# Two routed layers take their last rows in the order of arrival, and VectorE rotates the first two groups of a second attention

## What is computed

```
x += 0.5 * routed(LN(x))      # "routed0"
x += attn0(LN(x))             # low rank: state and action of 32, one head, causal
x += 0.5 * routed(LN(x))      # "routed1", the same weights
x += 0.5 * gated(LN(x))       # ternary weights with scales, 704 inner columns
x += attn1(LN(x))             # 16 heads of 128, rope, causal
x += 0.5 * gated(LN(x))
```

```
def routed(x):                # 16 experts, the best 4 of each token, at most 128 tokens per expert
    scores = softmax(x @ gate_w.T)
    topk_w, topk_i = top_k(scores, 4);  topk_w /= topk_w.sum(-1)
    ...                       # buf: for each expert the numbers of its tokens, wbuf: their weights
    xg   = xpad[buf]
    mid  = silu(xg @ w_gate) * (xg @ w_up)
    eout = (mid @ w_down) * wbuf[..., None]
    y    = zeros.at[buf].add(eout)
    shared = (silu(x @ sw_gate) * (x @ sw_up)) @ sw_down
    return y + shared

def rope(x):                  # on q and k of attn1
    x1, x2 = split(x, 2)
    return concat([x1 * c + x2 * s, -x1 * s + x2 * c])
```

## Time and profile before

| | us |
|---|---|
| median of three runs | 2019.42 |
| lowest and highest | 2014.98, 2020.13 |
| the profiled execution | 2020.47 |
| its span in the trace | 2018.7 |
| mean granted clock of TensorE in it | 0.992 |
| TensorE busy | 1938.0 (96%) |
| VectorE busy | 1435.0 (71%) |
| ScalarE busy | 1316.5 (65%) |
| GpSimd busy | 936.9 (46%) |

### The profile page before, as it was taken

The page is one execution under the profiler, slowest core; times in us unless marked ns, Lnnn a source line. Parts: engine busy times, 40 slices in busy tenths (PEclk is TensorE's granted clock), DMA queues, the critical chain, the costliest instruction groups (busy, mean ns, idle before and its releaser), DMA issues.

```text
span 2018.7 us, 40238 instructions
## 1 busy us (share of the span) xinstructions
PE 1938.0 (96%) x13726; PEld 1763.0 (87%) x13726; DVE 1435.0 (71%) x3587; ACT 1316.5 (65%) x3367; POOL 936.9 (46%) x961
## 2 busy tenths in 40 slices
PE   7988989898999999999999999999999999999999
PEld 5768867787899999999999999999999999998888
DVE  8368763755878777787877778787777878777753
ACT  4336633444778777777877777787777778776752
POOL 2641126444454536555453645545364554536242
PEclk9999989999999999999999999999999999999999
DMA  7750068500000000000000000000000000000000
GB/s 267 219 100 1 33 195 209 144 1 9 9 9 6 10 6 4 7 9 9 6 9 7 4 7 9 9 7 9 7 4 7 9 9 7 9 6 1 22 27 32
DMA packets 58600, 73.44 MB, mean 36 GB/s; under 512 B 9760, under 2 KB 45216, under 8 KB 58272
## 3 DMA queue, kind: packets, MB, share of 16 engines
q1 hardware_dynamic: 48032, 58.03, 8.9%
q0 software_dynamic: 10368, 12.85, 3.8%
HBM read 51.06 MB, written 19.80 MB: 35 GB/s over the span
## 4 chain that ended last, share of the span: by engine, by line
PE 61%; DVE 12%; ACT 9%; issue 7%; POOL 7%; DMA 4%; SPq 0%; ACTq 0%; POOLq 0%; DVEq 0%
PE phase_scores L1242 16%; PE phase_ring L1300 9%; PE phase_y L167 5%; PE phase_y L166 5%; PE phase_y L165 5%; PE phase_ring L165 4%; PE phase_ring L167 4%; PE phase_ring L166 4%; ACT phase_p L1274 3%; DMA y_rows<-phase_out,phase_rows 3%; DVE phase_scores L1253 2%; POOL phase_rot L2474 1%; POOL phase_straight L2472 1%; PE phase_up_ps L165 1%; PE phase_up_ps L167 1%
## 5 line engine op out<-in xcount | busy, mean ns | idle before, releaser
L1274 ACT ACTIVATE phase_p<-phase_scores,phase_bias 128x512 f32<-128x512 f32 (+3 forms) x680 | 417.5, 628 | 117.3 <-DVE phase_bias L1262 116.7
L1320 DVE TENSOR_TENSOR phase_pt_lo<-phase_ring,phase_pt_hi 128x512 fp32r<-128x512 f32 (+3 forms) x680 | 390.7, 604 | 90.1 <-ACT phase_pt_hi L1315 86.2
L1315 ACT ACTIVATE phase_pt_hi<-phase_ring 128x512 fp32r<-128x512 f32 (+3 forms) x680 | 343.1, 536 | 105.1 <-PE phase_ring L1300 100.8
L1300 PE MATMUL phase_ring<-sb_ident,phase_p 128*128 128x128 f32 x2312 | 340.7, 274 | 12.1 <-ACT phase_p L1274 6.7
L165 PE MATMUL phase_y<-phase_pt_hi,phase_v_hi 128*128 128x256 f32 (+1 forms) x1152 | 341.3, 296 | 6.5 <-DVE phase_y_lo L2448 6.3
L167 PE MATMUL phase_y<-phase_pt_hi,phase_v_lo 128*128 128x256 f32 (+1 forms) x1152 | 321.3, 279 | 0.0
L166 PE MATMUL phase_y<-phase_pt_lo,phase_v_hi 128*128 128x256 f32 (+1 forms) x1152 | 321.2, 279 | 0.0
L1300 PEld LDWEIGHTS phase_ring<-sb_ident,phase_p 128*128 128x128 f32 x2312 | 271.8, 140 | 53.3 <-ACT phase_p L1274 16.9
L1255 DVE TENSOR_REDUCE phase_peaks<-phase_scores 128x1 f32<-128x512 f32 (+1 forms) x408 | 265.8, 666 | 45.8 <-PE phase_scores L1242 43.5
L2472 POOL TENSOR_TENSOR phase_straight<-phase_rot,late_rope 64x512 f32<-64x512 f32 x128 | 163.7, 1279 | 275.5 <-ACT phase_rot L2341 275.4
L2489 POOL TENSOR_TENSOR sb_x<-sb_x,phase_part 128x512 f32<-128x512 f32 x128 | 164.8, 1288 | 253.4 <-ACT phase_part L2376 247.0
(11 more groups left out here) (282 smaller groups left out, 4848.8 us busy)
## 6 DMA issues: line engine op xcount, KB each, us to landing
phase_e_up<-expert_up SPq DMA_DIRECT2D x32, 352.0 KB, 4.7
phase_e_dn<-expert_down SPq DMA_DIRECT2D x32, 256.0 KB, 5.0
y_rows<-phase_zero SPq DMA_DIRECT2D x16, 512.0 KB, 7.8
xn_rows<-phase_ln_xn SPq DMA_DIRECT2D x8, 512.0 KB, 2.9
sb_x<-y_rows POOLq DMA_DIRECT2D x8, 512.0 KB, 6.6
late_raw_qk<-qk SPq DMA_DIRECT2D x16, 256.0 KB, 2.7
sb_x<-x SPq DMA_DIRECT2D x4, 512.0 KB, 5.6
phase_e_up<-y_rows SPq DMA_DIRECT2D x4, 512.0 KB, 4.5
```

Of the source, the lines that this page charges most:

```text
L1274: act.activation(self.p[:, at:at + width], self.scores[:, at:at + width], ACT.Exp, bias=self.bias[:, t % 2:t % 2 + 1], accum_out=self.sums ...
L1300: done = pe.transpose(bank[:, j * P:(j + 1) * P], self.p[:, (4 * place + j) * P:(4 * place + j + 1) * P], self.core.ident[:])
L1315: act.activation(hi, value, ACT.Copy).then_inc(*self.t_hi.one)
L1320: dve.tensor_tensor(lo, value, as_f32(hi), ALU.subtract).then_inc(*self.t_lo.one)
```

## The change

Five things change in the stages around the routed layers and in the opening of the second attention.

1. `AMONG, BEHIND` go from 6, 12 to 4, 14: two steps of the shared expert move from among the experts to behind them. The results get six rooms instead of four, so the weighing of n waits for scatter n-6. The two new rooms lie in memory that held `raw_dn` (first stage) or is new (second).
2. The tail is put in the order of arrival: SyncE fetches chunk 0 from both arrays, then chunk 1; `grow` follows that order, and the second array of chunk 1 is added after the sums of chunk 3 have begun. The norm of chunk 0 stays in the tail; of chunk 1 only the measuring does. Scaling and transposing chunk 1 become the follower's work: in Attention0 before its second projection, in Gated among its first pieces (`GROWN_NORM`), whose norms of chunks 2 and 3 come a few pieces later.
3. GpSimd in Attention0 and in the first Gated waits for the rows of chunk 1 before it issues any of the adding DMAs.
4. At the start of routed1 TensorE does piece `up` 0 right after `gate` 0 and `gate` 1 before the last logits are turned back; ScalarE does the rows of chunk 3 before the copies of logits. `rank` stands behind `gate` 2 there, before it stood in front.
5. In the second attention VectorE does the rotation (`rotate`) and the low parts (`part_qk`) for head 0, groups 0 and 1 (`OPENING`); the other 126 groups stay with GpSimd.

The core of the diff:

```diff
-    AMONG, BEHIND = 6, 12
+    AMONG, BEHIND = 4, 14
...
+        more_out = self.raw_dn[:, 0:2, :] if start else sb("out_more", [P, 2, H])[:]
+        self.out_rooms = [self.out[:, n, :] for n in range(4)] + [more_out[:, n, :] for n in range(2)]
...
-        among = {("sums", 1, 1): [("ahead", 0)], ("round", last - 3): [("ahead", 1), ("ahead", 2)], ("up", last - 2): [("ahead", 3), ("grow", 0, 0)],
-                 ("round", last - 2): [("grow", 1, 0)], ("up", last - 1): [("grow", 0, 1), ("measure", 0)], ("up", last): [("grow", 1, 1)],
-                 ("round", last): [("scale", 0)], ("sums", NCH - 2, 1): [("measure", 1), ("flip", 0, 0), ("flip", 0, 1)],
-                 ("sums", NCH - 1, 0): [("scale", 1)], ("sums", NCH - 1, 1): [("flip", 1, 0), ("flip", 1, 1)]}
+        among = {("up", last - 3): [("ahead", 0)], ("sums", 1, 1): [("ahead", 1)], ("round", last - 3): [("ahead", 2)], ("up", last - 2): [("ahead", 3)],
+                 ("round", last - 2): [("grow", 0, 0)], ("up", last - 1): [("grow", 0, 1), ("measure", 0)], ("round", last): [("grow", 1, 0), ("scale", 0)],
+                 ("sums", NCH - 2, 1): [("flip", 0, 0), ("flip", 0, 1)], ("sums", NCH - 1, 0): [("grow", 1, 1)], ("sums", NCH - 1, 1): [("measure", 1)]}
...
-        for b in range(2):
+        for c, b in ((0, 0), (0, 1), (1, 0), (1, 1)):
             sp.wait_ge(*self.placed[b][tag, NE - 2 + b])
-            for c in range(2):
-                rows = core.y_rows[b][c * CH:(c + 1) * CH, :]
-                sp.dma_start(self.y_rooms[c][b], rows.rearrange("(t p) h -> p t h", p=P)).then_inc(*self.y_fetched[c][b].one)
...
         if not self.start:
             self.pe_gate(pe, 0)
+            self.pe_multiplier(pe, 0)
...
         self.pe_logits(pe, 3)
+        if not self.start:
+            pe.wait_ge(*self.logits_out[tag, 2])
+            self.pe_gate(pe, 1)
         self.pe_logits_back(pe, (2, 3))
...
             elif what == "flip":
-                pe.wait_ge(*self.acted[tag, NCH * ISM - 1])
-                self.first.pe_flip(pe, *key, self.first_banks[key[0]][key[1]])
+                self.first.pe_flip(pe, *key, self.first_banks[key[1]])
...
-                if n >= 4:
-                    dve.wait_ge(*self.placed[n % 2][tag, n - 4])
+                if n >= 6:
+                    dve.wait_ge(*self.placed[n % 2][tag, n - 6])
...
     def pool(self, pool):
+        pool.wait_ge(*self.first.normed_v[self.tag, 1])
         for step in self.order:
...
+            pool.wait_ge(*self.first.normed_v[tag, 1])
             self.prior.pool_grow(pool, 0)
             self.prior.pool_grow(pool, 1)
...
-            order += [("rows", nc)] * (nc > 1) + [("bias", nc)]
+            order += [("rows", nc), ("bias", nc)]
...
-    GROWN_NORM = {(1, 0): [("scale", 0, 2)], (1, 1): [("turn", 0, 2)], (1, 3): [("scale", 0, 3)], (1, 4): [("turn", 0, 3)]}
-    GROWN_LATE = {(0, 4): [("measure", 0, 2), ("invert", 0, 2)], (1, 0): [("measure", 0, 3), ("invert", 0, 3)]}
+    GROWN_NORM = {(0, 1): [("scale", 2, 1)], (0, 2): [("turn", 2, 1)], (1, 2): [("scale", 0, 2)], (1, 3): [("turn", 0, 2)],
+                  (1, 4): [("scale", 0, 3)], (1, 5): [("turn", 0, 3)]}
+    GROWN_LATE = {(1, 0): [("measure", 0, 2), ("invert", 0, 2)], (1, 1): [("measure", 0, 3), ("invert", 0, 3)]}
...
+    OPENING = ((0, 0), (0, 1))
...
+                if key in self.OPENING:
+                    dve.wait_ge(*self.crossing[key])
+                    self.rotate(dve, key)
+            elif what == "finish" and key in self.OPENING:
+                self.part_qk(dve, key)
...
+    def rotate(self, engine, key):
+
+        wide = self.wide(slice(0, 64), key[1])
+        engine.wait_ge(*self.rotated[key])
+        engine.tensor_tensor(self.straight[:], self.rot[0:64], wide, ALU.mult).then_inc(*self.straightened.one)
+        engine.wait_ge(*self.straightened[key])
+        engine.tensor_tensor(self.rot[0:64], self.straight[:], self.crossed[:], ALU.add).then_inc(*self.turned_by_rope.one)
```

81 lines of the change are left out of this document (44 added, 37 removed).

## The result

| | us |
|---|---|
| before, median of five runs | 2018.71 |
| after, median of five runs (2026.58 to 2031.58) | 2029.88 |
| ratio, with its 95% interval | 1.006 (1.0047 to 1.0072) |
| the profiled execution after, its span | 2030.73, 2028.9 |

The forecast was 2017.3 with a range of 2008 to 2025. It missed by 12.6 us, to the slow side.

A forecast was written before the change was run, and what follows sets the result against it. TensorE, busy 96% of the span, was taken as the bound. Terms 0.3 + 3.6 - 0.7 - 1.1 = 2.1 us won, off the 2019.42 median, gave 2017.3, range 2008 to 2025.

The forecast's parts named there:

- first tail and Attention0: First routed tail through Attention0's opening: 3.6 us won less a 3.3 stall, net +0.3, bounds -5.8 and +3.6.
- opening of routed1: Start of the second routed stage: 3.1 us from TensorE's gaps and 0.5 from the clock, +3.6 won.
- second tail and gated stage: Second routed tail and gated stage: 3.9 us ahead from upstream, only 3.2 left later, so -0.7; bounds -6.8 and +2.2.
- rotation: Second attention's opening: first score some 1.8 us earlier, but VectorE's later statistics delay the softmax; -1.1, bounds -2.5 and +1.8.
- What bounds the kernel now: Whole kernel: TensorE is busy 96%; the change touches only stretches holding some 27 us of idle or low-clock time.
- Chunk 1 leaves the tail: First tail and Attention0: first projection about 6.0 us earlier; with 1.0 more, less 2.7 and 0.7, 3.6 won.
- GpSimd's new wait takes most of this back: Attention0: late additions of y make VectorE stand 3.3 us before the statistics of chunk 2.
- Rooms at nothing, two pieces at 1.0: First routed tail: six rooms win 0; two pieces behind the experts cut the gap before piece 11 to 2.7, winning 1.0.
- The bound of 5.1: Second routed stage's opening: upper bound of the gain in us, if the whole low-clock stretch goes.
- C: Rival: late additions of y land slowly, 12.7 us each, each stage 6.1 longer, 2029.5; decides from about 7.7; chance 0.15.

The follow-up runs named there:

- e13: e12 with the rows of chunk 1 scaled ahead of both values products in Attention0; 2012.98 us, 0.9979 to before.
- e14: e13 with the transposes of chunk 1 also ahead of the second values product in Attention0; 2011.34 us, 0.9969 to before.
- e8: The changed kernel with GpSimd's wait undone in Attention0 only, kept in the first gated stage; 2029.31 us, 1.0047 to before.
- e1: The changed kernel with GpSimd's waits for the rows of chunk 1 undone in Attention0 and the first gated stage; 2024.16 us, 1.0040 to before.
- e5: e1 with the rows of y fetched and added in the old order; 2024.05 us, 1.0032 to before.
- e9: e5 with chunk 1 scaled and turned in routed1's own tail and the gated stage's tables as before; 2018.77 us, 0.9998 to before.
- e7: The kernel before with the new opening of routed1 and six rooms for results; 2015.42 us, 0.9989 to before.
- e6: The kernel before with AMONG, BEHIND set to 4, 14 alone; 2016.56 us, 0.9994 to before.
- e2: The changed kernel with scaling and turning of chunk 1 back in the tails, and GpSimd's wait gone; 2031.45 us, 1.0072 to before.
- e12: e9 with the rotation of the first groups back on GpSimd; 2015.57 us, 0.9993 to before.
- e10: The kernel before with the new opening of routed1 and AMONG, BEHIND at 4, 14; 2015.63 us, 0.9989 to before.
- e3: The kernel before with the opening of routed1 alone, including the moved rank and gate 2; 2014.94 us, 0.9990 to before.

## Why the prediction was wrong, point by point

In the terms of the sum, after against before by the two traces: first tail and Attention0 +0.3 forecast and -4.7 measured, opening of routed1 +3.6 and +3.9, second tail and gated stage -0.7 and -7.5, rotation -1.1 and -1.5. The first and the third term are the miss.

- **"What bounds the kernel now" held.** Outside the six stretches little moved: the first fetch of routed0 came 0.8 later, and from the first turned chunk of Attention1 to the end it took 1513.1 before and 1513.4 after.
- **"Chunk 1 leaves the tail": this step failed, in the sentence "VectorE paces the opening of the attention, so of 6.0 + 1.0 I take off 2.7 and 0.7 for shifted waits".** It charged the norm of chunk 1 in the follower as VectorE's own time, and dropped the 1.94 of transposes that it had named. In the trace VectorE's time is 2.6, as I had it, but the stretch grew by 8.1, since rows, transposes, high and low parts and projection follow one another from VectorE and ScalarE to TensorE and back, each waited for the last, and the clock fell. e13 and e14 show that it was largely the place: the same work in another place costs less by 2.6 and 4.2 (medians). The gain in front is less certain: the first projection (139.40 before) came 2.2 earlier in the trace of after, 4.2 in e8 and 5.1 in e1, which have the same tail, and 5.8 in e5 with the old order of rows, where I had 6.0. The wait before chunk 0's transposes doesn't explain the 2.2: it is 2.57 there and 5.14 and 4.49 in e8 and e1. What does is open.
- **"Second tail and gated stage", -0.7: failed by 7.** This is the largest error. I took the same moves for the same small price and followed the queues only to the piece at 397.02, where I found the whole 3.2 ahead. Measured are +1.0 in front and -8.5 in the stage: 0.6 to 3.0 of it is GpSimd's wait (after and e8 against e1 and e5), the rest chunk 1's norm among the pieces together with the later norms of chunks 2 and 3 (e5 against e9, 8.7).
- **"GpSimd's new wait takes most of this back": right that it costs, wrong in the place.** I put a stall of 3.3 before the statistics of chunk 2. The second half of chunk 2 was issued at 153.73 and landed 7.7 later, at 161.5, where I had 6.6, but VectorE came there only at 161.84 and didn't wait. The same time was lost without GpSimd's wait (e1), so the chain hid it. In the gated stage, where I named the low halves queued behind it, it does cost.
- **Rooms at nothing, two pieces at 1.0: not contradicted.** e7 and e6 show no gain that can be measured; the one gap went to 1.57, another opened. In kernels with both parts the gap before piece 11 was not 2.7 but 4.35 (after, where the first rows of y came 2.1 later), 1.92 (e1) and 3.84 (e5). The earlier trace rows was misread here: the fetch of 4.36 from 116.13 serves the addition at 120.51, and the first addition, at 116.69, had waited for an earlier fetch.
- **Opening of routed1, +3.6: the sign held, the size is 2.1 between the means of all sixteen traces** (0.5 to 3.9 between single ones). The mean granted clock of the stretch rose from 0.85 and 0.89 before to 0.94; how much of the gain is the clock's and how much the gaps' was not separated. The bound of 5.1 was a slip: half of the 9.52 us of busy time is 4.8.
- **Rotation, -1.1: held in sign**, 1.5 to 2.1 lost; the first score came 1.44 earlier, not 1.8. The Trainium skill ("GPSIMD Engine Reference", "8. Key points") has VectorE about twice as fast for elementwise work, and it is, 0.68 against 1.28; the queue decided all the same.
- **The rivals.** C's 2029.5 is within 0.4 of the measured 2029.88 by luck, since its mechanism is not there: its landing of 12.7 did not come (least, median and most of the eight are 6.1, 6.6 and 8.4 after), and VectorE didn't wait for the 7.7 in Attention0, C's own threshold. The traces show more: the 12.7 belongs to the addition issued at 376.2, at the start of the gated stage. In each of the fourteen traces without GpSimd's wait in that stage the longest landing is 10.4 to 13.4, and in the two with it (after and e8) it is 8.4 and 8.0. No rival said that the moved norm itself is a chain, and my range, up to 2025, left C's figure out. Of the 0.17 for slower, 0.10 came from C.

The Trainium skill's rule of a shared interface ("GPSIMD Engine Reference", "8. Key points": contention with VectorE operations that have two inputs in SBUF) was left out of my sum. The traces agree with it: `dn_lo` with its two inputs in SBUF takes 0.41 at 383.58 with GpSimd idle and 3.84 at 392.49 beside low halves on GpSimd, and a 128x4 operation 3.53 in e2, as the 3.52 of the earlier trace rows. The long one of the earlier trace rows did go with the moved bias (0.15 in its place), and its like came back in the gated stage, which has no place in the forecast.

## What to carry to other kernels

Price a moved step by the chain that it opens, not by its engine time: go from the engine that makes its input to the one that needs its output, and see what stands ahead of each in its queue. A step that goes through several engines and back was cheap here only when it was started early in every queue, and moving it by a few places (e12 to e14, 4.2 us by the medians) was worth more than any other part of this change. And do the second place at which a change is made with the same care as the first: here the same move bought 5 to 8 in front of one stage and 1 to 3 in front of the other.

## What the runs showed of the hardware that I had not expected

- The stretch from the zeros to the first fetch of routed1 with the new opening takes one of two times, 29.3 (seven traces) or 30.9 (five), in kernels with the same code there; the mean granted clock over it is 0.94 in both. In e10 and e3 the low clock falls in different places: at 268.6 to 273.6 (0.66) in the short one, at 278 to 287.5 (0.79 and 0.85) in the long one. That the same loss of clock costs 1.6 us more where the chain runs through TensorE is my reading of these two traces; no run tests it.
- A VectorE subtraction of 128x256 that takes 0.41 at 383.58 took 3.84 beside two GpSimd subtractions of together 3.01, and 1.40 and 1.35 beside single ones of 1.29. What of this would go if they were kept apart was not tried.
